# Layer 1 of a two-layer graph network gathers from a table with a row per node and relation

## The reference, cut to what matters

```python
# layer 0
x_t = leaky(x @ W1n + b1n) @ W2n + b2n           # per node
e_t = leaky(edge_attr @ W1e + b1e) @ W2e + b2e   # per edge
agg = segment_sum(x_t[src] * e_t * dp_scale, dst)
x = layernorm(x + layernorm(x + agg * res_w) * gamma + beta)
# layer 1
rel_w = einsum('rb,bio->rio', w_comp, weight)    # 8 relations of 4 bases
xw = einsum('ni,rio->rno', x, rel_w)             # node times relation
msg = xw[etypes, src] * norm                     # norm: edge weight
x = layernorm(x + relu(segment_sum(msg, dst) + h_bias))
```

## Time and profile before

| what | us |
|---|---|
| median of 3 runs | 6131.65 (6127.79 to 6170.92) |
| profiled execution, its own time | 6124.1 |
| its span, first to last instruction | 6121.6 |
| POOL busy | 2973.2 (49% of the span) |
| PE busy, PE weight loads busy | 2740.4 (45%), 2374.4 (39%) |
| DVE busy | 2027.7 (33%) |
| ACT busy | 520.2 (8%) |
| mean granted PE clock | 0.673 of full |

### The profile page before, as it was taken

The page is one execution under the profiler, slowest core; times in us unless marked ns, Lnnn a source line. Parts: engine busy times, 40 slices in busy tenths (PEclk is TensorE's granted clock), DMA queues, the critical chain, the costliest instruction groups (busy, mean ns, idle before and its releaser), DMA issues.

```text
span 6121.6 us, 59899 instructions
## 1 busy us (share of the span) xinstructions
PE 2740.4 (45%) x14503; PEld 2374.4 (39%) x14504; DVE 2027.7 (33%) x3627; ACT 520.2 (8%) x1256; POOL 2973.2 (49%) x3194
## 2 busy tenths in 40 slices
PE   6555554545444444443434434434343344444434
PEld 5444443434333333333324433433343343444334
DVE  3222222323222222222234334334343343333334
ACT  2111111111111111111110000000000000000000
POOL 3555545454454444444445555454544544444442
PEclk7677666767666666666666676667676666666667
DMA  4111111111111111111101111010100110000110
GB/s 83 28 32 29 31 27 29 25 33 27 24 32 26 25 26 24 26 26 25 26 18 19 20 20 19 17 21 17 22 17 18 21 20 19 19 19 19 19 19 14
DMA packets 233733, 150.41 MB, mean 25 GB/s; under 512 B 129381, under 2 KB 181852, under 8 KB 233332
## 3 DMA queue, kind: packets, MB, share of 16 engines
q0 software_dynamic: 100096, 102.60, 8.8%
q1 hardware_dynamic: 132354, 44.29, 3.2%
q10 hardware_dynamic: 882, 0.13, 0.0%
HBM read 136.38 MB, written 10.42 MB: 24 GB/s over the span
## 4 chain that ended last, share of the span: by engine, by line
another core or an unknown queue 35%; PE 18%; issue 17%; DVE 16%; DVEq 10%; ACT 2%; DMA 0%; ACTq 0%; POOL 0%; POOLq 0%
PE ps_agg L1157 6%; DVEq L791 5%; DVE work L998 4%; DVE work L801 3%; PE ps_o L1142 3%; PE ps_agg L1151 3%; DVE hid L853 2%; PE ps_z L1130 2%; DVEq L810 2%; PE ps_fin L1240 1%; DVEq L815 1%; PE ps_o L1138 1%; DVEq L829 1%; DVE work L980 1%
## 5 line engine op out<-in xcount | busy, mean ns | idle before, releaser
L515 POOL DMA_INDIRECT rows<-node_table,src_ix x3128 | 2951.7, 944 | 3061.4 <-issue 985.2
L1157 PE MATMUL ps_agg<-work 128*128 128x128 f32 x6256 | 1147.2, 362 | 1618.8 <-DVE work L998 1328.9
L1157 PEld LDWEIGHTS ps_agg<-work 128*128 128x128 f32 x6256 | 1079.2, 270 | 1685.3 <-DVE work L998 1376.8
L815 DVE TENSOR_TENSOR acc<-acc,ps_agg 64x128 f32 (+1 forms) x782 | 272.3, 348 | 2539.6 <-remote 2004.2
L1138 PE MATMUL ps_o<-b2e,ones 3*128 3x256 bf16 x391 | 135.3, 346 | 1521.0 <-DVE hid L853 1263.1
L801 DVE TENSOR_TENSOR work<-ps_x,rel 128x512 f32<-128x512 f32 x782 | 541.0, 692 | 826.3 <-issue 553.7
L1138 PEld LDWEIGHTS ps_o<-b2e,ones 3*128 3x128 bf16 x391 | 37.3, 95 | 1628.6 <-DVE hid L853 1315.1
L1151 PE MATMUL ps_agg<-work 128*64 128x128 f32 x3128 | 572.3, 343 | 11.1 <-issue 10.6
L1151 PEld LDWEIGHTS ps_agg<-work 128*64 128x64 f32 x3128 | 455.9, 175 | 104.8 <-issue 93.3
L998 DVE TENSOR_TENSOR work<-rows,ps_z 128x1024 f32<-128x1024 f32 x391 | 473.3, 1211 | 10.6 <-DMA rows<-node_table,src_ix 10.6
L1142 PE MATMUL ps_o<-W2e_d,hid 128*128 128x128 f32 x1564 | 389.7, 390 | 0.0
(11 more groups left out here) (129 smaller groups left out, 1127.0 us busy)
## 6 DMA issues: line engine op xcount, KB each, us to landing
rows<-node_table,src_ix POOLq DMA_INDIRECT x3128
attr<-in_edge_attr_dram SPq DMA_DIRECT2D x78, 320.0 KB
node_table<-x_sb SPq DMA_DIRECT2D x14, 224.0 KB, 2.4
node_table<-work SPq DMA_DIRECT2D x24, 128.0 KB, 2.0
out_dram<-x_sb SPq DMA_DIRECT2D x13, 224.0 KB
src_ix<-src_groups SPq DMA_DIRECT2D x154, 10.0 KB
src_groups<-acc SPq DMA_DIRECT2D x1, 780.0 KB, 17.5
x_sb<-in_x_dram SPq DMA_DIRECT2D x1, 768.0 KB, 6.0
```

The costliest lines, as they stand in the source:

```text
L515: nc.gpsimd.indirect_dma_start(rows[0:n, slot_of(u), j, :], None, table, bass.IndirectOffsetOnAxis(ap=src_ix[0:n, half_of(u), col : col + ...
L815: return nc.vector.tensor_tensor(a, a, sums, ALU.add)
L1157: last = nc.tensor.matmul(bank[:, pr * P : (pr + 1) * P], scaled[:, ring, j, 2 * pr : 2 * pr + 2, :].rearrange("p b f -> p (b f)"), hot[:, ...
```

## The change

- The table between the layers, `rel_table`, has a row for each node and relation: the node's new features times that relation's 64x64 matrix `rel_w`. It is 8 times as large as `node_table2` was. `rel_w` is computed once by DVE before layer 0.
- It is written in layer 0, chunk by chunk. DVE's second layer norm writes to a buffer `fresh`. At the end of a body PE turns each of the 7 blocks (`ps_xT`) and multiplies it with `rel_w` (64x128 by 64x512), ACT copies the turned block and then the 128x512 product to `rel_rows`, and SP stores 7x512 floats per partition (1.8 MB per chunk; the last chunk block by block).
- Source and relation become one row number per edge, source times 8 plus relation, by DVE from PE's turned lists. It is stored by two further DMAs before layer 0.
- In layer 1 the gathered row is already the message without its weight. The weight sits in the one-hot: four `tensor_scalar` per tile (128x128 each, equal, then times weight) take the place of one `tensor_tensor` of 128x512, and `scale_rows` and the coefficients are gone. PE sums `rows` itself with four matmuls of 64 columns of weights. The sums are 64x128.
- The one-hots are made AHEAD - 1 = 4 tiles ahead of the add, in a ring of five, and PE has five banks. A slot is free when DVE has added the tile (`tile_done`), no longer when it has read the rows.
- At the end of layer 1 a chunk is only transposed, as in layer 0.
- SP's store of a layer-0 chunk waits for the products at the end of the body that holds the norm, and no longer for the norm.

```diff
--- before.py
+++ after.py
+    AHEAD = 5
...
-    node_table2 = nc.dram_tensor("node_table2", (NB * P, F), f32, kind="Internal").ap()
-    src_groups = nc.dram_tensor("src_groups", (FULL // GROUP, P, GROUP * J), i32, kind="Internal").ap()
+
+    rel_table = nc.dram_tensor("rel_table", (NB * P * R, F), f32, kind="Internal").ap()
+    src_groups, row_groups = (
+        nc.dram_tensor(name, (FULL // GROUP, P, GROUP * J), i32, kind="Internal").ap()
+        for name in ("src_groups", "row_groups")
+    )
+    row_tail = nc.dram_tensor("row_tail", (TAIL_P, J), i32, kind="Internal").ap()
...
+        onehot = work[:, at_w : at_w + AHEAD * J * P].rearrange("p (r j n) -> p r j n", r=AHEAD, j=J)
...
+        rel_rows = acc[:, 1, 0 : CH * R * F].rearrange("p (b q) -> p b q", b=CH)
+        fresh = acc[:, 1, CH * R * F : CH * (R + 1) * F].rearrange("p (b f) -> p b f", b=CH)
...
+        sums = [[ps_agg0, ps_agg1], [ps_agg0, ps_agg1, ps_o[0], ps_o[1], ps_z]]
...
+            def store_rel(c):
+
+                parts = [(b, b + 1) for b in range(CH)] if isinstance(c, int) else [(0, CH)]
+                for lo, hi in parts:
+                    sp.wait_ge(rel_staged, c * CH + hi)
+                    sp.sem_inc(loads_begun, 1)
+                    sp.dma_start(rel_chunks[c][:, lo:hi, :], rel_rows[:, lo:hi, :]).then_inc(table2_ready, 16)
...
-                    next_chunk(sp, done, limit, i + 1, lambda c: store_chunk(l, c))
+                    if l == 0:
+                        next_chunk(sp, done, limit, i, store_rel)
+                    else:
+                        next_chunk(sp, done, limit, i + 1, store_out)
...
+            sp.wait_ge(row_taken, 4)
+            sp.dma_start(
+                row_groups.rearrange("g p e -> p g e"),
+                row_ix[:, 0:FULL, :].rearrange("p (g s) j -> p g (s j)", s=GROUP),
+            ).then_inc(rows_stored, 16)
+            sp.dma_start(row_tail, row_ix[0:TAIL_P, FULL, :]).then_inc(rows_stored, 16)
...
-                table = (node_table, node_table2)[l]
+                table = (node_table, rel_table)[l]
                 if slot_used is not None:
 
-                    pool.wait_ge(msg_ready[l], slot_used)
+                    pool.wait_ge((msg_ready, tile_done)[l], slot_used)
...
+            def rel_copies(c):
+                act.wait_ge(normed[0], c + 1)
+                nc.scalar.copy(x_sb[:, bass.ds(c * CH, CH), :], fresh).then_inc(x_kept, 1)
+                act.wait_ge(table2_ready, c * 16)
+                act.sem_inc(copies_begun, 1)
+
+                def turned(b):
+                    act.wait_ge(x_turned, c * CH + (b + 1))
+                    nc.scalar.copy(xT[:, b % 2, :], ps_xT[0:F, :]).then_inc(xT_ready, 1)
+
+                turned(0)
+                for b in range(CH):
+                    if b + 1 < CH:
+                        turned(b + 1)
+                    act.wait_ge(rel_made, c * CH + (b + 1))
+                    nc.scalar.copy(rel_rows[:, b, :], ps_fin[:, :]).then_inc(rel_staged, 1)
...
+                next_chunk(act, tabled, limit, i, rel_copies)
...
+            def row_of(o, sources, types):
+                return nc.vector.scalar_tensor_tensor(o, sources, float(R), types, ALU.mult, ALU.add)
...
+            for b in range(B):
+                term = rel_terms if b else rel_w[:]
+                link(nc.vector.tensor_tensor(
+                    term,
+                    basis[:, b : b + 1, :].to_broadcast([F, R, F]),
+                    wcomp_r[0:F, :, b : b + 1].to_broadcast([F, R, F]),
+                    ALU.mult))
+                if b:
+                    link(nc.vector.tensor_tensor(rel_w[:], rel_w[:], rel_terms, ALU.add))
+            dve.sem_inc(rel_w_ready, 1)
...
-            def add_window(l, ring, k, bank):
-
-                nodes = bass.ds(dve.snap(window[ring]) + k * P, P)
-                if l == 0:
-                    a, sums = acc[0:F, 0, nodes], bank[0:F, 0:P]
-                else:
-                    a, sums = acc[:, :, nodes], bank[:, 0 : 2 * P].rearrange("p (q n) -> p q n", q=2)
-                return nc.vector.tensor_tensor(a, a, sums, ALU.add)
+            def add_window(ring, k, bank):
+
+                a = acc[0:F, 0, bass.ds(dve.snap(window[ring]) + k * P, P)]
+                return nc.vector.tensor_tensor(a, a, bank[0:F, 0:P], ALU.add)
 
             def add_sums(l, i, u, bank, last=False):
-                if last:
-
-                    dve.wait_ge(added[l], FULL + 1)
+                if last or l == 1:
+
+                    dve.wait_ge(added[l], tile_of(i, u) + 1)
                 dve.wait_ge(scattered[l], tile_of(i, u) + 1)
-                add_window(l, u % 2, 0, bank).then_inc(added[l], 1)
+                add_window(u % 2, 0, bank).then_inc(added[l], 1)
...
+            def weighted_hot(o, r, s):
+
+                weights = enorm[:, bass.ds(s, 1), :].rearrange("p o j -> p (o j)")
+                for j in range(J):
+                    last = nc.vector.tensor_scalar(
+                        o[:, j, :], iota_ps, r[:, j : j + 1], weights[:, j : j + 1], ALU.is_equal, ALU.mult)
+                return last
...
-            def coefficients(i, u):
-
-                h, tiles = half_of(u), bass.ds(tile_of(i, u), GROUP)
-                link_l(nc.vector.tensor_tensor(
-                    is_rel,
-                    etype[:, tiles, :].rearrange("p s j -> p (s j)").rearrange("p (e o) -> p e o", o=1).to_broadcast([P, GJ, R]),
-                    iota_ps[:, 0:R].rearrange("p (o r) -> p o r", o=1).to_broadcast([P, GJ, R]),
-                    ALU.is_equal))
-                link_l(nc.vector.tensor_tensor(
-                    is_rel, is_rel,
-                    enorm[:, tiles, :].rearrange("p s j -> p (s j)").rearrange("p (e o) -> p e o", o=1).to_broadcast([P, GJ, R]),
-                    ALU.mult))
-                link_l(nc.vector.tensor_tensor(
-                    coef_terms,
-                    is_rel.rearrange("p e (o r) -> p e o r", o=1).to_broadcast([P, GROUP * J, B, R]),
-                    wcomp_r[:].rearrange("p r b -> p b r").rearrange("p (o b) r -> p o b r", o=1).to_broadcast([P, GROUP * J, B, R]),
-                    ALU.mult))
-                link_l(nc.vector.tensor_reduce(coef[:, h, :, :], coef_terms, axis=AX.X, op=ALU.add))
...
-            def scale_rows(i, u, ring):
-                dve.wait_ge(gathered[1][slot_of(u)], uses(i, u) * ALL_GATHERS)
-                h, at = half_of(u), (u % GROUP) * J
-                nc.vector.tensor_tensor(
-                    scaled[:, ring, :, :, :],
-                    rows[:, slot_of(u), :, :].rearrange("p j (o f) -> p j o f", o=1).to_broadcast([P, J, B, F]),
-                    coef[:, h, at : at + J, :].rearrange("p j (b o) -> p j b o", o=1).to_broadcast([P, J, B, F]),
-                    ALU.mult,
-                ).then_inc(msg_ready[1], 1)
-
             def prepare1(i, u):
-                if u % GROUP == 0:
-                    coefficients(i, u)
-                main_one_hot(1, i, u)
-                scale_rows(i, u, u % 2)
+                s = tile_of(i, u)
+                weighted_hot(onehot[:, u % AHEAD, :, :], rel_of(s), s).then_inc(hot_ready, 1)
 
             def add_supertile1(i, u, last=False):
-                add_sums(1, i, u, ps_agg[u % 2], last)
+                span_of(i, u)
+                add_sums(1, i, u, sums[1][u % AHEAD], last)
                 extras(1, i, u)
-
-
-            dve.wait_ge(list_taken, 15)
+                dve.sem_inc(tile_done, 1)
+
+
+            dve.wait_ge(list_taken, 10)
             dve.wait_ge(chunk_zeroed, CHUNKS)
             dve.reg_mov(done, 0)
             dve.reg_mov(x_done, 0)
-            prepare1(0, 0)
+            for u in range(AHEAD - 1):
+                prepare1(0, u)
             with dve.Fori(0, BODIES - 1) as i:
                 for u in range(BODY):
-                    span_of(i, u)
-                    prepare1(i, u + 1)
+                    prepare1(i, u + AHEAD - 1)
...
+            def sum_by_target(data, hot, bank):
+                for j in range(J):
+                    last = nc.tensor.matmul(
+                        bank[0:F, 0:P], data[:, j, :], hot[:, j, :], start=(j == 0), stop=(j == J - 1)
+                    )
+                return last
+
+            def scatter(l, i, u):
+                s = tile_of(i, u)
+                pe.reg_load(further, control[0:1, bass.ds(s, 1), 0:1].rearrange("p o v -> p (o v)"))
+
                 if l == 0:
-                    for j in range(J):
-                        last = nc.tensor.matmul(
-                            bank[0:F, 0:P], msg[:, ring, j, :], hot[:, j, :], start=(j == 0), stop=(j == J - 1)
-                        )
-                    return last
-                for pr in range(2):
-                    for j in range(J):
-                        last = nc.tensor.matmul(
-                            bank[:, pr * P : (pr + 1) * P],
```

(39 more changed lines are left out.)

## The result

The kernel before took 6133.17 us (median of 4 runs, 6127.79 to 6170.92), the changed one **5950.14 us** (4 runs, 5937.77 to 5963.29): a ratio of 0.969, interval [0.9644, 0.9735]. The direction was right and the time lies in the stated range; of the 464 us that the forecast took off, 183 came. The profiled execution took 5937.77 us.

The account below looks back on a forecast made before the run. Bound: POOL pausing for slots while PE's completions come late in unbroken gather bursts. Layer 1's first gather at 3259 plus layer 1's 2399 gave a 5658 us span, with 2.5 around it 5660 us; range 5400 to 6030.

Parts of the forecast that it names:

- what is signalled before the spell can still be added in it: 9 tiles per burst: Layer 1: DVE adds 5 to 6 tiles, PE runs four ahead; 9 tiles per 50 us, 5.55 us per tile.
- the named bad case: Layer 1: only the five tiles made ahead are added per burst; 30 us for 5, 6.0 us per tile.
- VectorE's step: DVE's time per tile in layer 1: 1.40 us busy plus 0.9 for registers and branches, 2.3 us.
- Chunk pauses of layer 1: POOL's index-load waits behind SP's store and DVE's norm: 22 us each, 17 over an ordinary pause, 12 x 17 = 204 us.
- Products: Layer 0: turn, copy, product and copy follow each other, 2.8 us per block, 20 us per chunk without tiles.
- +7 us per chunk, 13 x 7 = 91: Layer 0, POOL's chunk pause: 35 us plus norms of 11, less 39 before; bounds -15 and +35 per chunk.
- The store: Layer 0: SP's 1792 KB store per chunk takes 12.8 us, with the index load behind it on the queue.
- Seam ... +20: Between the layers: the last chunk's seven products stand between norm and first gather; 3.3 us becomes 23.
- 1 (no pauses): Layer 1 has no pauses and is POOL's issue floor: 2180 us, total 5440; chance 12%.
- Rival 2: Layer 0's products fall into a burst and their signals come late: 28 us more per chunk, total 6020; chance 10%.
- Rival 3: Layer 1's `tensor_scalar` operations hold POOL's gather issue: 1.12 us more per tile, total 6100, no change; chance 5%.
- Rival 4: Layer 1 slots held too long: three tiles per burst, 8.3 us pause, 7.8 us per tile, total 6540; chance 7%.

Follow-up runs that it names:

- the narrow one-hots: Changed kernel with layer 1's four one-hot operations per tile writing 16 columns instead of 128: 5855.92 us, 0.958 of the kernel before.
- the later store: Changed kernel with SyncE waiting for a chunk's output one body of ten tiles later in layer 1: 5702.4 us, 0.935 of the kernel before.
- the base: The changed kernel run again unaltered, for comparison with the follow-up kernels: 5853.78 us, 0.957 of the kernel before.

## Why the prediction was right in sign and wrong in size

- **"what is signalled before the spell can still be added in it: 9 tiles per burst"** is the step that failed. The pause was right, 4.3 to 4.7 us for 5. But in the changed kernel's layer 1 VectorE's own queue is slow in the spell: one tile took it 14.2 us from add to add, so that in a burst hardly a tile is added once the spell has begun. Burst and pause are 24.1 us for 4 tiles, 6.03 us per tile for 5.55, or 391 x 0.48 = 188 us. This is the named bad case (6.0), reached with 4 tiles instead of 5, and bursts of 12 to 20 gathers were named as a sign of being wrong. Over the whole layer POOL's pauses came to 336 + 244 = 580 us, where the forecast has 391/9 = 43 of 5 us and 204 at the chunks, 421.
- **What could have been seen before.** Late signals were the right reading of the earlier trace rows for the kernel before: its trace has no slow queue on VectorE, and the earlier trace rows's signal at 4634.35. What did not follow is that ready signals make nine tiles. The 2.3 us per tile came from two adds without gathers, and was held to be true beside them. The trace of the kernel before would not have spoken against that, since its queue keeps its speed in a burst; the runs with the change do. And the cycle was drawn from a burst of 32 gathers behind a pause at a chunk, when the commonest was 16, before as after.
- **VectorE's step**: 2.3 us forecast, 2.37 measured outside the spell; the four one-hots take 1.37 for 1.12. Outside the spell the value was near and did not matter: the narrow one-hots show that VectorE's work could shrink further for nothing.
- **Chunk pauses of layer 1**: 22 us forecast, 20.3 measured, and the cause as stated: the later store takes them all away.
- **Products**: 2.8 us a block forecast, 2.75 measured. **"+7 us per chunk, 13 x 7 = 91"** was mis-sized: layer 0's last gather moved from 3106 to 3292 us; 11 of these 186 us lie before the tiles (10 forecast), so 175/13 = 13.5 per chunk. I had POOL's pause end with store and index load on SyncE's queue. The store's wait had been moved a body later by the same change (the diff shows `i` for `i + 1`), so that pause all but vanished, and the products' 20 us instead fell into the ring, where no slot came free. In the base's trace the last gather is 78 us earlier, at 3214, which leaves 97/13 = 7.5 per chunk against the same trace of the kernel before: near the 7 forecast, but by the other route, so that is luck.
- **The store**: 12.8 us forecast, 6.4 measured. The 3.6/544 us per KB was drawn from two rows of other stores.
- **"Seam ... +20"**: it was +61 (92.7 us from gather to gather for 31.6). Two sets of products stand in it: those of the last chunk but one come at the end of the last body, when POOL has no gather left to issue.
- The sum: layer 0 +126 us over its forecast, layer 1 +152, together the 278 us by which 5936 lies above the 5658 forecast for the span. The forecast's own bounds, 5480 to 5840, do not follow from the terms given for them: 5.3 to 6.0 us per tile and -10 to +15 us per chunk add up to 5341 to 5940.
- **Rivals.** 1 (no pauses) is false where it was asked; on the chips without spells POOL's issue is all there is of layer 1. Rival 2 was a part of the truth, smaller and for another reason: no pause of layer 0 reached 60 us. Rival 3 is false: a gather takes 944 ns with `tensor_scalar` beside it. The Trainium skill, VectorE: DVE Perf Modes, "Why PSUM operands drop a tier", had spoken against it, and these rows agree. Rival 4 had the bursts of 4 tiles right and the pause (8.3 us for 4.3 to 4.7) wrong, and with it the sign; it named slots that are freed late, and freeing them earlier gained nothing.

## What to carry to other kernels

Where an engine's chain says "queue", "issue" or "remote" while the engine that it waits for is done, look at how long its register, branch and semaphore instructions take at that moment: in the changed kernel they were slow, in the kernel before they were not and the signal was late. The same word stood for both. Look again after a change, since what held the engine up before need not be what holds it up now. Take the cycle that you cost from the commonest burst, counted over the whole layer, and not from one timeline. Before costing a load, look at what stands ahead of it in its queue: moving one wait by one body gave 151 us, where 180 us less of VectorE's arithmetic gave nothing. And a change that is 3 to 4% faster on one chip can be 3% slower on the next: price the parts on both.

## What the runs showed of the hardware

- In layer 1 of the changed kernel and its variants, in unbroken bursts of indirect gathers, instructions that VectorE's queue executes itself came to take 0.70 us or 1.40, mostly from 6 to 8 us after the burst's start until 2 to 4 us after the last gather's; memsets and one-hots beside them kept their 0.03 and 0.41 us. Of instructions of 0.65 to 0.76 us in layer 1, SyncE's queue had 49 to 203 in these runs, TensorE's 0 to 86, ScalarE's 0 to 18. In both layers of the kernel before and in layer 0 of the changed one VectorE's queue had hardly any (1 of 5635, 11 of 5752).
- On other chips the kernel before took 4045 us for 6110, and three variants of the changed one 4168 to 4171 for 5702 to 5775 (two of them), without a pause of POOL in layer 1.
- TensorE's granted clock was 0.53 in the changed kernel's layer 1 and 0.66 in its layer 0, where it does more: in layer 1 almost always its lower level, 1.2 GHz. Before, with twice the matmuls in layer 1, it was 0.67 there.
- Writing fewer columns shortens little: `tensor_scalar` of 128x16 took 290 ns, of 128x128 405.
